# Causal attention between two mixture-of-experts layers: weighing two key tiles in a row instead of one

## What is computed

```python
x = x + 0.5 * ffn(layernorm(x), router_w, w1, w2, w3)
x = x + attn(layernorm(x), wq, wk, wv, wo)
x = x + 0.5 * ffn(layernorm(x), router_w, w1, w2, w3)

# attn: 16 query heads, 4 key/value heads, head width 32, rotary embedding, causal
attn = einsum('bhqd,bhkd->bhqk', q, k) / sqrt(HD)
attn = softmax(where(mask, -inf, attn), axis=-1)
out = einsum('bhqk,bhkd->bhqd', attn, v)
```

## Time and profile before

| | |
|---|---|
| three runs | 1319.73, 1323.73, 1327.27 us |
| the profiled execution, its own time | 1328.63 us |
| its span | 1327.4 us |
| mean granted TensorE clock (of full speed) | 0.966 |
| PE busy, share of the span | 89% |
| DVE / ACT / POOL busy | 68% / 50% / 45% |

### The profile page before, as it was taken

One profiled execution on the slowest core, in us unless ns is written; L12 is line 12 of the kernel. 1 busy time (PEld: TensorE's weight loads), 2 busy tenths in 40 slices (PEclk: granted clock), 3 DMA queues, 4 the chain that ended last, 5 costly groups with the idle time before them and its releaser, 6 DMA issues.

```text
span 1327.4 us, 21769 instructions
## 1 busy us (share of the span) xinstructions
PE 1185.9 (89%) x7252; PEld 771.0 (58%) x7252; DVE 906.8 (68%) x2104; ACT 661.6 (50%) x1313; POOL 595.8 (45%) x495
## 2 busy tenths in 40 slices
PE   4489999959998999999989999999998848999996
PEld 3468888838776554455445554445543336777774
DVE  7867777759996666576577776587645475666664
ACT  2535555526455554364365555365566633444442
POOL 4544444314110111001436645547491363877876
PEclk9689999979999999999999999999999978999999
DMA  9823333366530032024245745557541352666665
GB/s 333 332 80 108 108 112 110 122 167 113 88 61 6 30 67 34 1 97 68 61 128 144 154 114 127 152 140 159 129 93 37 112 198 69 102 100 99 98 98 75
DMA packets 66971, 146.92 MB, mean 111 GB/s; under 512 B 8784, under 2 KB 28240, under 8 KB 62864
## 3 DMA queue, kind: packets, MB, share of 16 engines
q0 software_dynamic: 35184, 93.34, 33.5%
q1 hardware_dynamic: 31680, 52.19, 11.4%
HBM read 79.71 MB, written 33.55 MB: 85 GB/s over the span
## 4 chain that ended last, share of the span: by engine, by line
PE 59%; DVE 17%; DMA 9%; issue 7%; POOL 5%; ACT 3%; SPq 0%; POOLq 0%; DVEq 0%; ACTq 0%
PE bank L827 9%; PE bank L1586 9%; PE bank L1598 9%; PE bank L984 8%; PE bank L850 5%; DMA out<-Y,DI 4%; PE bank L1614 4%; PE bank L1651 3%; DVE PM L997 3%; DMA XG<-xn,TK 3%; POOL out L777 3%; DVE bank L999 2%; PE bank L809 2%; PE bank L722 1%; PE bank L1376 1%
## 5 line engine op out<-in xcount | busy, mean ns | idle before, releaser
L1699 ACT ACTIVATE P<-bank 128x512 f32<-128x512 f32 (+3 forms) x640 | 304.8, 535 | 271.7 <-PE bank L1586 265.8
L997 DVE TENSOR_REDUCE PM<-bank 128x1 f32<-128x512 f32 x384 | 253.1, 686 | 85.9 <-PE bank L984 85.1
L1586 PE MATMUL bank<-Qs,Ks 98*128 98x512 f32 (+3 forms) x640 | 246.0, 409 | 8.9 <-ACT P L1699 7.3
L984 PE MATMUL bank<-Ks,Qs 96*128 96x512 f32 (+3 forms) x640 | 238.0, 390 | 13.9 <-DVE PM L999 6.4
L1586 PEld LDWEIGHTS bank<-Qs,Ks 98*128 98x128 f32 x640 | 116.7, 189 | 141.0 <-ACT P L1699 67.5
L1738 POOL TENSOR_SCALAR_AFFINE_SELECT P<-P 128x512 f32<-128x512 f32 x64 | 41.9, 655 | 299.8 <-ACT P L1699 250.1
L999 DVE CUSTOM_DVE_ANT_0 bank<-bank,KB 128x128 f32<-128x128 f32 (+3 forms) x256 | 124.7, 498 | 55.0 <-PE bank L984 54.5
L984 PEld LDWEIGHTS bank<-Ks,Qs 96*128 96x128 f32 x640 | 120.3, 189 | 71.0 <-DVE PM L997 26.9
L1598 PE MATMUL bank<-P,V 128*32 128x512 f32 (+3 forms) x1280 | 149.9, 539 | 0.3 <-ACT P L1699 0.2
L777 POOL DMA_INDIRECT out<-Y,DI x78 | 127.3, 1632 | 44.7 <-issue 31.8
L1752 POOL TENSOR_TENSOR CH<-CH,P 128x512 f32<-128x512 f32 x108 | 138.0, 1393 | 16.9 <-ACT P L1699 16.3
(11 more groups left out here) (193 smaller groups left out, 1949.4 us busy)
## 6 DMA issues: line engine op xcount, KB each, us to landing
CD<-P POOLq DMA_DIRECT2D x17, 1024.0 KB, 7.1
xn<-XN SPq DMA_DIRECT2D x8, 1024.0 KB, 6.5
WR<-L_ffn_w POOLq DMA_DIRECT2D x16, 512.0 KB, 15.2
XO<-y POOLq DMA_DIRECT2D x8, 1024.0 KB, 9.4
WR<-L_ffn_w SPq DMA_DIRECT2D x16, 512.0 KB, 7.8
CD<-P SPq DMA_DIRECT2D x7, 1024.0 KB, 5.0
CD<-CH POOLq DMA_DIRECT2D x7, 1024.0 KB, 8.2
XA<-y POOLq DMA_DIRECT2D x24, 256.0 KB, 4.2
```

The source lines that it names most:

```text
L984: pe.matmul(bk(g, bank)[:, 0:n], g.Qs[b][0:96, G % 4 * 4 + h, c * P:c * P + P], g.Ks[0:96, G % 4, k * BQ:k * BQ + n], start=True, stop=Tru ...
L997: dve.tensor_reduce(dst, bk(g, bank)[:, 0:n], AX.X, ALU.max).then_inc(s(f"free{bank}"), 1)
L1586: pe.matmul(bk(g, i % 3)[:, o:BQ], g.Ks[0:98, G % 4, k * P:k * P + P], g.Qs[G // 4][0:98, G % 4 * 4 + j, o:BQ], start=True, stop=True).the ...
L1699: act.activation(a.P4[buffer_of(n)][:, j, o:BQ], bk(g, i % 3)[:, o:BQ], ACT.Exp, scale=scale).then_inc(s("exp"), 1)
```

## The change

A new function `weighed_with(n)` says which tiles are weighed behind the scores that follow tile `n`. In groups 0 to 7 it is tile `n` itself, as before. In groups 8 to 15 it is nothing for an even `k`, and tiles `n - 1` and `n` for an odd `k`. `solvemax` and `found` stand in the same branch, so that in these groups they too can only come where a pair is weighed. The slice in which finish steps are looked for grows from 8 to 12 steps.

```diff
+def weighed_with(n):
+
+    G, k = TILES[n]
+    if G < 8:
+        return [n]
+    return [n - 1, n] if k % 2 else []
...
-            if j == 3 and n:
+            if j == 3 and n and weighed_with(n - 1):
                 if known and known[0][0] <= at and free and n - 1 not in LAST.values():
                     copying.append(known.pop(0)[1])
                     plan.append(("solvemax", copying[0]))
-                plan.append(("weigh", n - 1))
+                plan += [("weigh", m) for m in weighed_with(n - 1)]
                 if copying:
                     plan.append(("found", copying[0]))
...
-            for step in [p for p in plan[-8:] if p[0] == "finish"]:
+            for step in [p for p in plan[-12:] if p[0] == "finish"]:
...
-    plan += [("weigh", len(TILES) - 1), ("out", 15), ("up1", 4), ("split1", 0), ("split1", 1), ("split1", 2), ("tsum", 15), ("even", 15)]
+    plan += [("weigh", m) for m in weighed_with(len(TILES) - 1)]
+    plan += [("out", 15), ("up1", 4), ("split1", 0), ("split1", 1), ("split1", 2), ("tsum", 15), ("even", 15)]
```

## The result

| | before | the change |
|---|---|---|
| first seven runs of each, median | 1322.60 us | 1334.91 us |
| lowest to highest | 1319.73 to 1328.63 | 1331.10 to 1339.24 |
| the profiled execution, its own time | 1328.63 us | 1339.24 us |
| mean granted TensorE clock in it | 0.966 | 0.957 |

The ratio is 1.0072 (95% interval 1.0050 to 1.0094): the change makes the kernel slower by 0.7%, where I forecast 0.3% faster and gave "slower by over 0.5%" a chance of 0.13. Measured again, the change was 7.5 us above before (1333.73 against 1326.19) where it was 12.3 us above it here (1334.91 against 1322.60): the sign repeats, the size is known to a few us only.

The account below looks back on a forecast made before the run. PE was taken as the bound, with savings and VectorE's refills nearly cancelling: 2.4 + 3.5 - 5.2 - 2.3 + 2.0 - 4.2 = -3.8 us, rounded to -4. Against the median 1323.7 that gave 1319.7 us, range 1306 to 1331.

Parts of the forecast that it names:

- what bounds the kernel now: Opening step: PE, busy 89% of the span and at full clock in the attention, is the bound.
- `tsum` and `even`: Seven cycles where PE's extra work lets VectorE catch up: 0.3 us saved in each.
- `found`: Seven waits of PE for `solvemax`, 0.7 us in the mean, nearly vanish: 7 x 0.6 = -4.2 us.
- pure cycles: Twelve cycles with tops and nothing else, where VectorE's refill swallows the saving: +0.2 us each, +2.4.
- VectorE's work: Seven cycles with statistics, scaling or `best` on VectorE, no longer hidden under PE: +0.5 us each, +3.5.
- The replay of tiles 7 and 8 of group 13: One cycle with tops, worked through in the new order: 6.68 us, before 6.63.
- the projection's cycles: Four cycles with the projection, where PE's extra work gives VectorE time: 0.4 us saved in each.
- the diagonal ones with tops: Nine diagonal cycles with short scores and long blocks keep half the saving: 9 x 0.25 = -2.3 us.
- PE's waits for tops' banks: Sign in the profile after: up from almost nothing to about 0.3 us a cycle or more.
- case 4: Rival: a weigh behind a weigh saves nothing at its end, +6.7 us on the sum, 1326.4 us; chance 0.12.
- Costs nothing: Three `found` moving a tile later cost nothing, since their maxima are wanted groups later.
- The third case: Rival: dearer VectorE refill in all 44 cycles with tops, +19.8 us, 1339.5 us in all; chance 0.13.

Follow-up runs that it names:

- e4: The change, with the maximum of a 512-column top taken over its first 128 columns only: 1299.06 us, before 1324.11.
- e5: The kernel before, with the maximum of a 512-column top taken over its first 128 columns only: 1300.77 us, before 1325.02.
- e6: The kernel before with single weighs, but `solvemax` and `found` only where the change allows them: 1324.84 us, before 1325.02.
- e1: The change without pairs in three cycles, those with the long waits: 1328.57 us, before 1324.11.
- e9: The change with a copy in place of the layer norm's square root inside the attention: 1329.23 us, before 1325.02.
- e12: The change with each tile's first top ahead of its first score in groups 8 to 15: 1330.94 us, before 1326.19.
- e3: The change with pairs only in the 22 cycles that had been shorter with them than before: 1317.51 us, before 1324.11.
- e7: e3 with the tops' lead held at 32 scores by weight: 1316.92 us, before 1325.02.
- e8: e3 with each tile's first top ahead of its first score in groups 8 to 15: 1315.70 us, before 1326.19.

## Why the prediction was wrong

- **The clock, the step that failed.** Under "what bounds the kernel now" I took the full clock, 1.00, for a property of the stage and carried it into every case; none of my four had a clock that falls. It depends on the order, and even before's order lost it once in its second trace. The change keeps PE's work but gathers its waits, and in group 15 its stretches at ScalarE's pace. This took 14.1 us in six cycles. About 4.3 of them are the waits themselves (2.37 against 1.34 us in (8, 11), 2.08 against none in (11, 11), 2.24 against 1.03 in (12, 11)); the larger part is the halved clock, at 1.3 to 1.6 us for each 3.4. In the other three cycles no new long wait explains the fall: in the 6 us ahead of it PE waited for at most 0.46 us in (12, 9), 0.21 in (13, 5) and 0.22 in (15, 9). What brought it on in the first two is not shown, and in the second trace they kept the clock. The Trainium skill (TensorE: Matmul & The Clock Gate, "Part 1: The HAM clock gate") says that the chip grants TensorE's clock by how busy it has been. The traces agree in the direction, and they add that a stage need not be idle to lose it: PE is busy for 417.5 of 440 us between 590 and 1030 us in the change and for 418.2 in before, with 0.97 and 1.00 of the clock.
- **The sum at a full clock came out close, partly by errors that cancel:** -3.8 forecast for 56 cycles, -3.0 and -3.3 measured in the 49 and 50 that kept the clock in the two traces, -2.1 in the 52 that kept it in at least one. Its terms: `tsum` and `even` 7 x 0.3 forecast, 2.3 us in sum measured; `found` 4.2 forecast, 4.7 measured in five cycles, with what those changed otherwise; a pair in group 15 5.45 us forecast, 5.43 measured; pure cycles +0.2 each forecast, +0.1 measured in eight; VectorE's work +0.5 each, +0.4 to +0.6 measured. The replay of tiles 7 and 8 of group 13 gave 6.68 us, and with 0.45 for `found` (0.1 of waiting, 0.35 to the next score) 7.13; the trace has 7.10.
- **Wrong within the sum:** the projection's cycles gain nothing but where `found` lies in them ((8, 3) +0.01, (12, 3) +0.06, (12, 5) +0.18, forecast -0.4 each); the diagonal ones with tops gain 0.8 us in eight instead of 2.3; those at the end, set at 0, gain 0.8, and (14, 9) loses 1.0, for which I have no reason. Of the cycles with turns, set at -0.3 each, (9, 3) and (9, 7) are 0.4 and 0.2 us longer. And one sign that I named hardly showed: PE's waits for tops' banks (L984 for L997 and L999) went from 1.8 to 6.0 us in all, 2.2 of them a single wait, so 0.1 us a cycle and not 0.3.
- **The weigh behind a weigh** takes 0.88 us, as I had set it, and saves the change of mode, 0.3 us (case 4 falls); e4 against e5 shows the saving without VectorE's limit. The Trainium skill (TensorEngine Tiling, "Key Properties") has that drain, and the runs agree: 0.3 us for each one spared.
- **"Costs nothing"** for the later `found` was true alone (e6) and false with the pairs.
- **The third case** had the right sign for another reason. It wanted at least 0.24 us more in each of the 44 cycles with tops; the 39 at full clock in both traces had 4.4 us less together.
- In the account of the kernel before, the denominators of tile 11 in groups 12 to 14 are PE's too, five tiles and not four; the replayed cycles don't hold it, since both were read up to the weigh.

What stays open: what makes the clock fall where PE has no long wait, as in group 15, and why it held in before's (8, 11) once with a wait of 1.34 us and not the next time. That waits and falls go together is shown over 14 traces; that a wait brings the fall on was tried by taking a wait away in one cycle only. The falls of e1 to e9 and e12 rest on one trace each.

## What to carry to other kernels

Gathering TensorE's small pieces of work saves its changes of mode (0.3 us each here) but gathers its waits too; where other engines set the pace, the saving is theirs to swallow, so pair only in the places where TensorE is late itself (e3: the same edit in 22 of 56 places turned +0.7% into -0.5%). Before costing a reordering of TensorE's work, look at the granted clock as something that the order earns: compare cycles that differ in nothing but the clock, and count a new long wait on PE as costing a slower stretch too: here each of the 19 of 1.45 us or more did, and only seven of the 41 near one microsecond. And two harmless changes (a `found` later, a score earlier) can make a wait between them that neither makes alone.

## What was not expected of the hardware

TensorE's clock fell to half in a stage where TensorE was busy 95% of the time, for 3.4 or 6.8 us at a time, with no wait above 0.22 us ahead of it in group 15. Versions whose cycles were shorter at a full clock often lost more of it: e5 had 13.7 us at half clock in groups 8 to 15 where before had 0 and 3.4, e7 and e8 had 13.7 and 6.8 where e3 had 0. Most cycles at the same clock repeat to 0.02 us from execution to execution.
